# Cross-attention and ternary FFN in one kernel: another order of the first tiles' steps, weight sums and first w2 loads

## What is computed

```
x = x + attention(layernorm(x), ctx)              # one row of attn per x row
h = layernorm(layernorm(x), gamma, beta)
xq = round(h * 127 / max|h| per row)              # int8 range
w1q = clip(round(w1 / mean|w1|), -1, 1)           # one mean over all of w1; w2 alike
h = gelu(xq @ w1q.T / scales + b1)                # 512 -> 2048
hq = round(h * 127 / max|h| per row)
x = x + hq @ w2q.T / scales + b2                  # 2048 -> 512
```

## Time and profile before

| | before |
|---|---|
| median of 3 runs | 541.45 us (538.63 to 542.35) |
| profiled execution | 540.51 us, span 538.7 us, mean granted clock 0.99 |
| busy: PE, DVE, ACT, POOL | 98, 84, 81, 76% of the span |
| DMA, first 40 us (three slices) | 8 to 9 tenths busy or more, 310 to 402 GB/s |
| `second_layer(0)` starts | 80.81 us |

### The profile page before, as it was taken

One profiled execution on the slowest core, in us unless ns is written; L12 is line 12 of the kernel. 1 busy time (PEld: TensorE's weight loads), 2 busy tenths in 40 slices (PEclk: granted clock), 3 DMA queues, 4 the chain that ended last, 5 costly groups with the idle time before them and its releaser, 6 DMA issues.

```text
span 538.7 us, 8129 instructions
## 1 busy us (share of the span) xinstructions
PE 527.3 (98%) x2434; PEld 227.4 (42%) x2434; DVE 453.6 (84%) x758; ACT 435.9 (81%) x444; POOL 407.3 (76%) x533
## 2 busy tenths in 40 slices
PE   9979989999999999999999999999999999999997
PEld 5433434444444444444444444444444444444443
DVE  3877999999989899988888887988888889887653
ACT  3558899888887888888888888888888889887762
POOL 2288687999998888888888988888888888873300
PEclk9987999999999999999999999999999999999999
DMA  8999233886565656555665556665455574535433
GB/s 310 402 387 294 69 69 102 170 208 162 135 122 141 131 148 119 129 125 130 131 143 142 123 129 117 141 132 132 124 123 130 129 142 103 92 86 100 95 78 98
DMA packets 137015, 78.72 MB, mean 146 GB/s; under 512 B 114246, under 2 KB 114310, under 8 KB 136972
## 3 DMA queue, kind: packets, MB, share of 16 engines
q1 hardware_dynamic: 135636, 75.80, 57.3%
q10 hardware_dynamic: 1335, 2.41, 1.3%
HBM read 33.88 MB, written 17.05 MB: 95 GB/s over the span
## 4 chain that ended last, share of the span: by engine, by line
PE 95%; DVE 3%; POOL 1%; ACT 1%; issue 1%; POOLq 0%; DVEq 0%; ACTq 0%
PE py L1055 41%; PE p L1040 28%; PE pab L1040 14%; PE p L983 3%; PE p L1030 3%; PE pab L1008 2%; PE pab L1030 1%; POOL xr L387 1%; PE pab L968 1%; DVE hx L792 1%; PE py L1016 1%; PE py L1008 1%; DVE w2q L779 1%; ACT hid L578 0%; PE py L974 0%
## 5 line engine op out<-in xcount | busy, mean ns | idle before, releaser
L1055 PE MATMUL py<-w2q,hqT 128*128 128x512 bf16 x1024 | 231.0, 379 | 1.7 <-DVE hqT L829 1.7
L587 ACT ACTIVATE hq<-hid,hscale 128x2048 int8<-128x2048 f32 x64 | 128.1, 2002 | 46.2 <-DVE hscale L821 46.2
L1040 PE MATMUL p<-w1q,xqT 128*128 128x512 bf16 x688 | 159.4, 380 | 0.0
L1055 PEld LDWEIGHTS py<-w2q,hqT 128*128 128x128 bf16 x1024 | 100.1, 98 | 123.0 <-DVE hqT L829 2.7
L578 ACT ACTIVATE hid<-p,xdeq 128x1024 f32<-128x1024 f32 x86 | 95.0, 1106 | 15.9 <-PE p L1040 11.2
L1040 PEld LDWEIGHTS p<-w1q,xqT 128*128 128x128 bf16 x688 | 63.8, 98 | 81.2 <-issue 10.1
L387 POOL TENSOR_TENSOR xr<-xr,attn 128x512 f32<-128x512 f32 x64 | 83.3, 1320 | 18.7 <-DVE attn L727 17.2
L402 POOL TENSOR_TENSOR hx<-hx,beta_b 128x512 f32<-128x512 f32 x64 | 91.7, 1454 | 4.4 <-ACT hx L563 4.3
L815 DVE TENSOR_REDUCE hmax<-hid 128x1 f32<-128x1025 f32 x64 | 78.1, 1220 | 18.0 <-ACT hid L578 17.4
L406 POOL TENSOR_TENSOR xr<-xr,b_b 128x512 f32<-128x512 f32 x64 | 92.6, 1465 | 0.0
L809 DVE TENSOR_REDUCE hid<-hid 128x1 f32<-128x1024 f32 x64 | 77.4, 1209 | 8.8 <-ACT hid L578 8.8
(11 more groups left out here) (88 smaller groups left out, 408.9 us busy)
## 6 DMA issues: line engine op xcount, KB each, us to landing
xr<-x SPq DMA_DIRECT2D x64, 256.0 KB, 2.9
...
raw<-w1T SPq DMA_DIRECT2D x8, 512.0 KB, 12.2
...
wout<-w2T SPq DMA_DIRECT2D x3, 512.0 KB, 5.5
xr<-w2T SPq DMA_DIRECT2D x2, 512.0 KB, 11.1
...
```

Source lines behind the costliest of these rows:

```text
L587: nc.scalar.activation(hq8[:, t % 2, :], hid[:, t % 2, 0:HID], ACT.Copy, scale=col(hscale, t))\
L1040: mm = nc.tensor.matmul(hidden_bank(t, n), xT[:, k, :], w1q[:, k, n * D:(n + 1) * D], start=False, stop=(k == KD - 1))
L1055: mm = nc.tensor.matmul(py[:, t % 2, :], hqT[:, t % 2, c // 2, c % 2, :], w2q[:, c, :], start=(c == 0), stop=(c == 2 * NJ - 1))
```

## The change

All arithmetic stays but for one detail: which engine takes a sum of absolute values. ScalarE sums all eight pieces of |w1| (two of them were VectorE's); VectorE sums pieces 0 and 1 of |w2| (ScalarE did). `load_w2(0)` to `load_w2(4)` are issued from ScalarE's list, the others stay with SP. The context's load goes ahead of x tiles 4 to 6, w1's last two pieces ahead of x tile 3. On TensorE, `first_layer(0)` goes ahead of `out_rows(2)`, `weight_total(1)` between the halves of `first_layer(1)`, and `out_rows` waits for the copies of Wv Wout one by one. On ScalarE, VectorE, GpSimd and SP the calls of the ramp are in another order. In the hunks of ScalarE's and VectorE's lists the removed lines are left out; the lines with a plus or a blank are the new list.

```
@@ -207,8 +207,6 @@
             .then_inc(w1_loaded[i], 16)
     def load_w2(j):
-        if j == 3:
-            sp.wait_ge(mean_done, 1)
         if j == 5:
             sp.wait_ge(wvo_done, KD)
         sp.dma_start(w2raw[j], w2T[j * 2 * P:(j + 1) * 2 * P, :].rearrange("(p e) n -> p e n", e=2))\
@@ -286,40 +284,35 @@
     load_w1(4)
     load_w1(5)
     sp.dma_start(beta_b[:, :], beta.partition_broadcast(P)).then_inc(beta_loaded, 16)
-    load_x(3)
     load_w1(6)
     load_w1(7)
+    load_x(3)
+    load_ctx()
+    load_b1_rows()
     load_x(4)
-    load_w2(0)
-    load_b1_rows()
     load_x(5)
-    load_w2(1)
-    load_ctx()
-    load_w2(2)
     load_x(6)
-    load_w2(3)
-    load_w2(4)
     transpose_x(0)
     load_w2(5)
     load_w2(6)
+    transpose_x(1)
     load_w2(7)
     load_x(7)
     load_x(8)
     load_x(9)
+    transpose_x(2)
+    transpose_x(3)
     sp.dma_start(b2_b[:, 0, :], b2.partition_broadcast(P)).then_inc(b2_loaded, 16)
     load_x(10)
-    transpose_x(1)
     load_x(11)
     load_x(12)
     load_x(13)
-    transpose_x(2)
-    transpose_x(3)
+    transpose_h(0)
+    load_x(14)
+    load_x(15)
+    transpose_h(1)
     transpose_x(4)
-    transpose_h(0)
     transpose_x(5)
-    load_x(14)
-    transpose_h(1)
-    load_x(15)
     transpose_h(2)
     sp.wait_ge(tail_copied, 1)
     sp.dma_start(tail_rows, tail_out).then_inc(tail_stored, 16)
@@ -440,37 +433,37 @@
     pool.wait_ge(mean_copied, 1)
     add_attention(0, 1)
     add_attention(1, 1)
-    add_attention(2, 1)
-    add_attention(3, 1)
     pool.wait_ge(const_set, 3)
     inverse_std(0, 1)
+    add_attention(2, 1)
     inverse_std(1, 1)
     pool.wait_ge(beta_loaded, 16)
     add_beta(0, 1)
-    inverse_std(2, 2)
-    add_attention(4, 1)
     add_beta(1, 1)
-    add_attention(5, 1)
+    add_attention(3, 1)
     widen_x(0, 1)
     pool.wait_ge(wscale_done[0], 1)
     scale_rows(0, 1)
+    inverse_std(2, 2)
+    widen_x(1, 1)
+    scale_rows(1, 1)
     add_beta(2, 1)
     add_beta(3, 1)
+    add_attention(4, 1)
+    scale_rows(2, 2)
+    add_attention(5, 1)
+    add_attention(6, 1)
+    widen_x(2, 2)
     inverse_std(4, 2)
-    scale_rows(1, 1)
-    add_attention(6, 1)
-    widen_x(1, 1)
+    add_attention(7, 1)
     add_beta(4, 1)
     add_beta(5, 1)
-    scale_rows(2, 2)
-    widen_x(2, 2)
-    add_attention(7, 1)
     add_attention(8, 1)
     scale_rows(4, 2)
     add_attention(9, 1)
+    inverse_std(6, 2)
     pool.wait_ge(b2_loaded, 16)
     add_b2(0)
-    inverse_std(6, 2)
     add_attention(10, 1)
     add_attention(11, 1)
     widen_x(4, 2)
@@ -526,6 +519,13 @@
     for m in range(KI):
         act.dma_start(wout[:, m, :], wout_d[m * P:(m + 1) * P, :]).then_inc(chunk_loaded[m], 16)
+    def load_w2(j):
+        if j == 3:
+            act.wait_ge(mean_done, 1)
+        act.dma_start(w2raw[j], w2T[j * 2 * P:(j + 1) * 2 * P, :].rearrange("(p e) n -> p e n", e=2))\
+            .then_inc(w2_loaded[j], 16)
+
+
     def first_gelu():
         act.wait_ge(const_set, 2)
         nc.scalar.activation(wpart[:, 0, 6:8], neg_half[:, :], ACT.Gelu).then_inc(vmean_done, 1)
@@ -606,69 +606,74 @@
     mean_sum(5)
     mean_sum(6)
     mean_sum(7)
+    abs_w1(0)
     abs_w1(1)
     copy_wvo(0)
     abs_w1(2)
     copy_wvo(1)
     abs_w1(3)
+    abs_w1(4)
     times_std(0)
     abs_w1(5)
+    times_std(1)
+    load_w2(0)
+    abs_w1(6)
+    load_w2(1)
     copy_wvo(2)
...
     abs_w1(7)
+    load_w2(2)
     round_x(0)
+    load_w2(3)
+    round_x(1)
+    load_w2(4)
+    round_weights(0, 1)
+    copy_wvo(3)
+    round_weights(0, 3)
     times_std(2)
     times_std(3)
...
+    abs_w2(2)
+    abs_w2(3)
+    abs_w2(4)
+    gelu(0, 0)
+    abs_w2(5)
+    gelu(0, 1)
+    abs_w2(6)
+    abs_w2(7)
+    round_x(2)
+    round_x(3)
+    gelu(1, 0)
+    round_weights(1, 0)
+    gelu(1, 1)
+    round_weights(1, 1)
     times_std(4)
     times_std(5)
...
     round_h(0)
     round_weights(1, 2)
     round_weights(1, 3)
+    gelu(2, 0)
     round_weights(1, 4)
...
     gelu(2, 1)
...
     round_weights(1, 5)
     round_weights(1, 6)
+    round_h(1)
+    round_x(4)
+    round_x(5)
     widen_h(0)
     round_weights(1, 7)
...
     gelu(3, 0)
     gelu(3, 1)
     round_h(2)
     widen_h(1)
+    times_std(6)
+    times_std(7)
     gelu(4, 0)
+    round_h(3)
+    gelu(4, 1)
     round_x(6)
     round_x(7)
...
+    widen_h(2)
     times_std(8)
...
     times_std(9)
...
     gelu(5, 0)
     round_h(4)
     gelu(5, 1)
@@ -745,16 +750,15 @@
         dve.wait_ge(tail_done, 1)
         nc.vector.tensor_tensor(tail_out, py[0:NB, 0, :], bout_b[0:NB, :], ALU.add).then_inc(tail_copied, 1)
-    def abs_w1(i):
-        k, h = i // 2, i % 2
-        dve.wait_ge(w1_loaded[i], 16)
-        nc.vector.tensor_reduce(wpart[:, 0, i:i + 1], raw1[:, k, h * HALF:(h + 1) * HALF], AX.X, ALU.add,
+    def abs_w2(n):
+        dve.wait_ge(w2_loaded[n], 16)
+        nc.vector.tensor_reduce(wpart[:, 1, n:n + 1], w2raw[n], AX.XY, ALU.add,
                                 apply_absolute_value=True).then_inc(wabs_dve, 1)
     def weight_sum(j):
-        if j == 0:
+        if j == 1:
             dve.wait_ge(wabs_dve, 2)
-        dve.wait_ge(wabs_act[j], (6, 8)[j])
+        dve.wait_ge(wabs_act[j], (8, 6)[j])
         nc.vector.tensor_reduce(wsum[:, j:j + 1], wpart[:, j, :], AX.X, ALU.add).then_inc(wsum_done[j], 1)
     def weight_scale(j):
@@ -860,84 +864,84 @@
     mean_weighted(6)
     mean_weighted(7)
     mean_row()
...
     statistics(0)
     dve.wait_ge(gamma_loaded, 16)
     centre(0)
     statistics(1)
+    centre(1)
     statistics(2)
...
     centre(2)
     x_scale(0, 1)
+    weight_sum(0)
+    x_scale(1, 1)
+    weight_scale(0)
+    round_w1(0)
+    clip(0, 0)
+    statistics(3)
     centre(3)
...
+    clip(0, 1)
     round_w1(2)
...
     clip(0, 2)
     clip(0, 3)
+    attn_rows(0)
+    abs_w2(0)
+    abs_w2(1)
+    ctx_sum(0)
+    x_scale(2, 2)
+    ctx_sum(1)
     attn_rows(1)
+    half_scale(0)
+    ctx_sum(2)
+    statistics(4)
+    hidden_scale(0)
+    centre(4)
+    ctx_sum(3)
+    statistics(5)
+    weight_sum(1)
+    centre(5)
+    weight_scale(1)
     attn_rows(2)
...
+    half_scale(1)
     ctx_means()
...
+    hidden_scale(1)
+    clip(1, 0)
+    clip(1, 1)
     x_scale(4, 2)
...
+    attn_rows(3)
     statistics(6)
     statistics(7)
...
+    clip(1, 2)
+    clip(1, 3)
+    half_scale(2)
+    hidden_scale(2)
+    clip(1, 4)
+    tail_rows_out()
+    clip(1, 5)
+    widen_h(0)
+    clip(1, 6)
+    clip(1, 7)
+    half_scale(3)
+    widen_h(1)
+    centre(6)
+    hidden_scale(3)
+    centre(7)
     statistics(8)
     statistics(9)
...
+    x_scale(6, 2)
+    half_scale(4)
     centre(8)
...
     result(0)
...
     widen_h(2)
     hidden_scale(4)
+    centre(9)
+    statistics(10)
+    statistics(11)
     result(1)
+    half_scale(5)
     centre(10)
+    hidden_scale(5)
+    x_scale(8, 2)
     centre(11)
...
     widen_h(3)
     for s in range(6, T + LAG + 1):
@@ -998,13 +1002,13 @@
     def out_rows(i):
         b = (i + 1) % B
-        pe.wait_ge(wvo_copied, KD)
         if i == 2:
             pe.wait_ge(attn_copied, 1)
         if i == 3:
             pe.wait_ge(wmean_done[1], 1)
         pe.wait_ge(ctxm_loaded, 16 * KD)
         for k in range(KD):
+            pe.wait_ge(wvo_copied, k + 1)
             mm = nc.tensor.matmul(row_banks[i], ctxm[k][:, b * P:(b + 1) * P], wvo[:, k, :],
                                   start=(k == 0), stop=(k == KD - 1))
         mm.then_inc(attn_done, 1)
@@ -1067,12 +1071,12 @@
     out_rows(0)
     out_rows(1)
     bias(0)
-    out_rows(2)
     first_layer(0, 0)
     first_layer(0, 1)
-    weight_total(1)
+    out_rows(2)
     bias(1)
     first_layer(1, 0)
+    weight_total(1)
     first_layer(1, 1)
     out_rows(3)
     bias(2)
```

More of the change, by code:

```diff
@@ L663, in _ @@
             widen_h(1)
+            times_std(6)
+            times_std(7)
             gelu(4, 0)
+            round_h(3)
+            gelu(4, 1)
             round_x(6)
             round_x(7)
-            gelu(4, 1)
+            widen_h(2)
             times_std(8)
-            widen_h(2)
             times_std(9)
-            round_h(3)
             gelu(5, 0)
@@ L886, in _ @@
-            attn_rows(0)
-            ctx_sum(3)
-            round_w1(0)
+            weight_sum(0)
+            x_scale(1, 1)
+            weight_scale(0)
+            round_w1(0)
+            clip(0, 0)
+            statistics(3)
+            centre(3)
+            clip(0, 1)
             round_w1(2)
-            clip(0, 0)
-            clip(0, 1)
             clip(0, 2)
             clip(0, 3)
-            attn_rows(1)
+            attn_rows(0)
+            abs_w2(0)
+            abs_w2(1)
@@ L895, in _ @@
+            ctx_sum(0)
+            x_scale(2, 2)
+            ctx_sum(1)
+            attn_rows(1)
+            half_scale(0)
+            ctx_sum(2)
+            statistics(4)
+            hidden_scale(0)
+            centre(4)
+            ctx_sum(3)
+            statistics(5)
+            weight_sum(1)
```

(64 more changed lines are left out.)

146 lines of the change are left out of this document (65 added, 81 removed).

## The result

The changed kernel is slower: its runs have a median of 546.99 us (544.64 to 547.57, 4 runs) beside 540.04 us (537.97 to 542.35, 4 runs) for the kernel before, a ratio of 1.0119 with a 95% interval of 1.0061 to 1.0177. (The ratio is worked out from all the runs, so it stands 0.1% off that of the two medians.) Its profiled execution took 546.44 us, with a span of 544.6 (before 538.7). The forecast was 549.8, so its direction and its main step were right and its time was 2.8 us too high; the time is that of rival 1.

A forecast was written before the change was run, and what follows sets the result against it. TensorE (527.3 of 538.7 us busy) was taken as the bound; an earlier second layer (1.9 us), a 6.7 us wait at `bias(6)` and half clock behind it put `second_layer(3)` +8.4 later: 541.45 to 549.8, range 545 to 554.

The forecast's parts named there:

- main step: At `bias(6)`: TensorE stands 6.7 us because tile 11's statistics on VectorE come late and GpSimd holds tile 6 behind them.
- rival 1: Tile 6 late, but no clock fall at `weight_total(1)`, whose wait is 1.7 us: +4.0 to +5.5, 546.5 us; chance 0.2.
- What bounds, and where to look: TensorE, busy 527.3 of 538.7 us; the forecast is when `second_layer(3)` starts (103.03 before), with 435.7 us from there on.
- The wait for |w1| goes: Before the first `weight_total`: the 3.5 us wait vanishes, the clock stays full, products end at 36.4 instead of 41.8.
- The new wait at `weight_total(1)`: Between `first_layer(1)`'s halves: TensorE waits 3.7 us (1.7 to 5) for VectorE's `weight_sum(1)`; clock falls, 7 in 10.
- Start of the second layer: `second_layer(0)` starts at 78.9 (76.2 without the clock fall) instead of 80.81, a gain of 1.9 or 4.6 us.
- The x chain of tiles 6 and 7: VectorE's tile 11 statistics at 96.9 delay GpSimd's tile 6; its transpose lands at 103.7 and `bias(6)` waits 6.7 us.
- And behind that: GpSimd's later list delays tile 3's half to 109.5, hidden by half clock after `bias(6)`; `second_layer(3)` at 110.6 to 111.5.
- The sum that left every fall of the clock out: Both predicted waits, at `weight_total(1)` and `bias(6)`, cost only their own length, with no half clock: 546 us.
- Rival 2: Tiles 6 and 7: the x chain isn't late and the ramp's gain of 1.9 to 4.6 stays: 537 to 539.5; chance 0.1.
- Rival 3: VectorE's steps stretch beside GpSimd, `weight_total(1)` at 58.7, tile 11's statistics 3 us later: +11 to +12, 553; chance 0.15.
- rival 4: w1's last sum is late, so the first wait stays and all behind moves by 1 to 3 us: 552; chance 0.05.

## Why the prediction was right or wrong

**What bounds, and where to look.** Right. From `second_layer(3)` to the end nothing changed (435.6 and 435.7 us), and the whole difference was the start of this one call. Of the 2.8 us that the time was too high, 1.4 are its base: it added 8.4 us to a median of 541.45 over 3 runs, and with a fourth the median is 540.04. Between the medians are 7.0 us, between the profiled executions 5.9.

**The wait for |w1| goes.** Right: no wait, full clock, `out_rows(0)` at 37.83 (predicted 36.9). ScalarE's last sum ended at 34.5 and VectorE's sum behind it at 34.7 (33.4 and 33.6 had been expected), though the DMA issues took 0.33 to 0.39 us and not 0.6; it was in time all the same, since the products ahead of `weight_total(0)` ended at 36.0 and not at 34.2.

**The new wait at `weight_total(1)`.** Right in place and releaser, wrong in size, and this is the term that failed. I took 22.4 us from `weight_scale(0)` to `weight_sum(1)`, between 20.4 and 23.7; it was 20.1, just under the short end. (The short end itself was added up wrong: its terms give 21.4, not 20.4.) The four clips, for which I had taken some 0.9 each, took 0.69, 0.69 and 1.59 for two; `round_w1` 1.32 and 1.28 rather than 1.75. Most of the 2.3 us that the list was shorter went again, because it began later, `weight_scale(0)` being done at 36.6 and not at 34.8; and TensorE came to `weight_total(1)` at 54.3 and not at 53.6. So the wait was 2.56 us, not 3.7, and in it the clock did not fall, to which I had given 3 in 10. Without that spell the sum is rival 1's: 546.5. Its range was added up wrong as well: 2.8 us off the forecast's +7.6 to +9.2 is +4.8 to +6.4, not +4.0 to +5.5; measured were +5.9.

**Start of the second layer.** 76.40, where the sum without the fall gave 76.2. Not foreseen: TensorE waits 2.75 us there and the clock falls now, for some 3 us, so `second_layer(0)` takes 5.09 us in place of 3.63. I had priced falls only for the two waits I named. It should have cost nothing in the end, since tile 6's date hung on VectorE's list: with 1.5 us less here `bias(6)` would have waited 1.5 longer. No run tested this.

**The x chain of tiles 6 and 7.** The main step, and right: who waits for whom is as predicted. From `widen_h(0)`'s end at 76.3 to tile 11's statistics at 95.1 are 18.8 us, predicted 16.7 without a wait and 19.2 with one. That 19.2 was so near is partly luck: the wait of `half_scale(3)` for a GELU, which made it, never came. The 2.1 us over 16.7 are two clips that took 2.90 us beside GpSimd in place of 1.4, and 0.66 us of waiting for GpSimd at `x_scale(6, 2)`. From there to the end of `widen_x(6, 2)` 4.0 (4.0), the transpose 2.7 (2.7), the wait 5.6 (6.7; 4.6 was given as the least). `bias(6)` at 101.79, predicted 103.7.

**And behind that.** The list behind `widen_x(6, 2)` took 5.1 us (5.3 to 7) and a half-clock spell came as predicted. `widen_h(3)` took 1.76 us beside GpSimd's work, where I had some 0.6, so tile 3 came 9.7 us behind `widen_x`, not 8.5. That the two blocks hide each other was right; the start of `second_layer(3)` moved by +5.95. `bias(8)` wasn't late.

**The clock.** The sum that left every fall of the clock out, 546, was nearer than mine, for another reason: a spell did come at `bias(6)`, but behind a block that hid most of it. A fall to half was seen in or behind every wait of 2.91 us or more in these traces and in none of 2.56 or less; in between it went either way (last section). By the Trainium skill (TensorE: Matmul & The Clock Gate, The HAM clock gate) an idle array drops to half rate; the trace agrees, with the lengths just given.

**Rivals.** Rival 2 (not late, the ramp's gain stays) fell. But its price was wrong too: I had the change's front worth 2 to 5 us by itself. The two kernels that have it without the late chain are at ratios of 1.0017 and 0.9996. Rival 3's long list is refuted by 20.1; rival 4 by the missing first wait.

**What is shown and what is argued.** Shown: moving tile 11's and tile 10's statistics alone costs the old kernel 1.2%; putting the chain back takes the changed kernel's loss away; two blocks lie behind each other, and curing one shifts the wait to the other. Argued: that the ramp as a whole is held by VectorE's list (72 of its 81 us busy), so that TensorE's earlier waits are free. Two things speak for it: the old kernel with its sums moved, where TensorE ends its products 4.4 us earlier (37.48 against 41.84) and the median is the same, and the 5.90 us wait that costs nothing in the kernel with the chain put back. One speaks against it, the kernel before itself: of its 23 runs beside these two, the nine with a mean granted clock of 0.996 or more took 537.95 to 539.31 us, the seven with 0.991 or less 541.13 to 542.09. The kernel with its sums moved took 539.38 to 539.82 in its seven runs at 0.997 or more, above the former and below the latter. So time at half clock goes with up to 3 us in the old kernel and isn't all free there, come from an execution with a long spell (540.51 us, 0.99), and the level medians may hide a gain and a loss. Open: this, why 2.4 us less work on VectorE gave 1.2, and which part of VectorE's remaining 8 to 9 us of idle time (3.3 of it for GpSimd's adds) could go.
